# ScalarE's loop back-edge moved from between groups to between the second and third tile of a group

## The chip, the core and the metric

The kernel runs on one core of a Trainium2 chip. The metric is device time in microseconds. Five engines run their own instruction streams and meet at semaphores only: TensorE (PE), VectorE (DVE), ScalarE (ACT), GpSimd (POOL) and SyncE (SP), which issues most DMAs. Before the change the kernel takes 840.57 us, the median of three runs (840.33 to 841.09).

## The reference, cut to what matters

512 samples each look up 32 embedding rows of 32 numbers. Two layers of a compressed interaction network follow, and then a small dense network.

```python
for W in filters:                                  # two layers, 128 maps each
    z = einsum('bhd,bmd->bhmd', x0, prev)          # x0: 512 x 32 x 32
    cur = relu(einsum('bpd,pn->bnd', z.reshape(b, h * m, d), W[0]))
    prev = cur; outs.append(cur)
z = sum(concatenate(outs, axis=1), axis=-1)
h = relu(concatenate([z, dense_ctx], axis=1) @ W_top1 + b_top1)
y = relu(h @ W_top2 + b_top2) @ W_top3
```

Nearly all of the work is the second layer: for every sample, place d, field h of 32 and map n, a sum over 128 maps of the first layer, multiplied by the embedding x0[b, h, d], and then summed over h.

## The kernel before, in words

The samples are cut into 128 tiles of four samples (128 rows of sample and place), and four tiles make a group (`TG` is 4), so there are 32 groups. For each tile, PE computes the second layer's product before the multiplication by the embedding: eight banks of PSUM, k from 0 to 7, each with four fields of 128 maps. One bank takes three matmuls of 512 columns (`layer1`, L921, L922, L929: high and low halves of float32 numbers). PSUM has six such banks in a ring (`RING`). PE writes bank n only when the reader of bank n-6 is done; those are the waits at L910 and L911, on `act_scaled` and `dve_scaled`.

ACT reads five of a tile's eight banks (k = 0, 1, 3, 5, 6): four instructions a bank multiply 128x128 by the embedding and write `prod` (`scale`, L577). DVE reads the other three (k = 2, 4, 7), and adds its products onto ACT's of the bank named in `PARTNER` (L746), so that it waits for ACT as well. POOL folds `prod` (L447), and DVE reduces the rest of it (L758).

Between these, each engine makes ready the next groups. The first layer of the next group is 13 matmuls of PE in each group, three in the second tile and ten in the third (`Z_USED_AT`, L972). ACT has, in a group, five instructions `split_z` (L538; three in the first tile, two in the second), one `rectify_parts` (L561, `c_parts`, at the end of the second tile) and one `rectify_hi` (L555, in the fourth tile). So ACT's extra work stands in the first two tiles of a group and PE's in the third.

All engines run `over_groups` (L103). Groups 0 and 1 are written out. Groups 2 to 28 are a loop of nine iterations with three groups each, and groups 29 to 31 are written out again. The order of work of each engine is the order of the code in `body`; there is no scheduler. At the end of an iteration each engine's own sequencer adds one to the loop's register and branches back (L108), eight times. Nothing makes the engines turn over together, apart from the semaphores of the work. In the stream of ACT the loop is 375 instructions, in that of DVE 317.

Of the kernel before, what the change touches and what calls it, by code (L numbers as in the profile page):

```python
# [39 lines left out]
TG = 4  # L40
# [8 lines left out]
SLOTS = 3  # L49
# [50 lines left out]
        engine.wait_ge(semaphore, value)  # L100


def over_groups(engine, body):  # L103

    body(Group(0, 0), 0)
    body(Group(0, 1), 1)
    loops = (GROUPS - 2) // SLOTS - 1
    with engine.Fori(0, loops) as i:  # L108
        for r in range(2, 2 + SLOTS):
            body(Group(i, r), None)  # L110
    for g in range(2 + SLOTS * loops, GROUPS):
        body(Group(g // SLOTS, g % SLOTS), g)


LAST = Group((GROUPS - 1) // SLOTS, (GROUPS - 1) % SLOTS)
# [2 lines left out]
def tower(nc, ids_and_bounds, copy_of, ones_of_b, picks, table, dense_x, dense_w, w0a, w0b, w1, wt1, wt2, bt2, wt3, y):  # L118
    ctx = ExitStack()
    with ctx:  # L120
# [193 lines left out]
        def _(sp):  # L314
# [76 lines left out]
            def body(g, number):  # L391
                if number is None or number > 1:
                    write_h1(g.plus(-2))
                if number is None or number + SLOTS < GROUPS:
                    send(g.plus(SLOTS), number is None or number + SLOTS + 1 < GROUPS)
                    fetch(g.plus(SLOTS))

            over_groups(sp, body)
            for s in range(SLOTS):
                sp.wait_ge(h1_written[s], 16 * BT * (len(range(s, GROUPS - 2, SLOTS)) + 1))  # L400
# [7 lines left out]
        def _(pool):  # L408
# [64 lines left out]
            def body(g, number):  # L473
                more = number is None or number + 1 < GROUPS
                folds_late = number is None or number < GROUPS - 1
                for u in range(TG):
# [49 lines left out]
                    if (number, u) == (GROUPS - 2, 3):  # L526
                        nc.gpsimd.tensor_copy(dense_x_r[:, :], dense_x_sb[:, :]).then_inc(top_hi_ready, 1)
                        nc.gpsimd.tensor_copy(dense_w_r[:, :], dense_w_sb[:, :]).then_inc(top_hi_ready, 1)

            over_groups(pool, body)  # L530

        @block.scalar
        def _(act):
            def split_z(g, k):

                act.wait_ge(z_ready, g.times(KP, k + 1))
                wait(act, l0_done, g.times(1))
                nc.scalar.activation(z_hi[:, k, :], z[:, k, :], ACT.Copy,  # L538
                                     scale=copy_sb[:, 0:1] if k == LASTK else 1.0).then_inc(z_hi_ready, splits_at_once(g))

            def round_z(tiles, hi_ready, count):

                nc.scalar.activation(by_tile(z_hi[:, LASTK, :])[:, tiles], by_tile(z[:, LASTK, :])[:, tiles], ACT.Copy,
                                     scale=copy_sb[:, 0:1]).then_inc(hi_ready, count)

            def rectify_first(at, out_of, hi_ready):

                nc.scalar.activation(c_hi[:, 0, at], out_of[:, at], ACT.Relu).then_inc(hi_ready, 1)

            def rectify_hi(g):  # L550

                act.wait_ge(l0_done, g.times(1, 1))
                if not isinstance(g.i, int) or g.i > 0:
                    act.wait_ge(h0_done, g.times(1, 1 - SLOTS))
                nc.scalar.activation(c_hi[:, g.r, :], ps_c[:, :], ACT.Relu).then_inc(c_hi_ready, 1)  # L555

            def rectify_parts(g):

                act.wait_ge(reduced, g.times(TG * HALVES, TG * HALVES))
                wait(act, c1_ready, g.times(1))  # L560
                nc.scalar.activation(c1_parts[:, :, :], csum[:, g.r, :, :], ACT.Relu).then_inc(parts_rectified, 1)  # L561

            def rectify_end(u):

                act.wait_ge(reduced, LAST.times(TG * HALVES, (u + 1) * HALVES))
                nc.scalar.activation(c1_end[:, u, :], csum[:, LAST.r, :, u], ACT.Relu).then_inc(end_rectified, 1)

            def scale(g, u, k):

                if k == ACT_BANKS[u][0]:  # L570
                    if u == 0:
                        act.wait_ge(es_ready, g.times(1, 1))
                    wait(act, reduced, g.times(TG * HALVES, (u + 1 - BUFS) * HALVES))
                act.wait_ge(y_ready, g.times(TG * NK, u * NK + k + 1))
                for j in range(HB):
                    h, place = HB * k + j, place_of(u, k) + j
                    last = nc.scalar.activation(prod[:, buffer_of(g, u), place // 2, :, place % 2],  # L577
                                                ps_y[:, bank_of(g, u, k), j * N:(j + 1) * N], ACT.Copy,
                                                scale=es[:, g.r, u, h:h + 1])
                last.then_inc(act_scaled, 1)  # L580

            def round_w1(banks):

                for k in banks:
                    act.wait_ge(w1_in[k * W1_LOADS // NK], 16)
                    nc.scalar.activation(w1_hi[:, k * HB:(k + 1) * HB, :], w1_raw[:, k * HB:(k + 1) * HB, :],
                                         ACT.Copy).then_inc(w1_hi_ready, 1)
# [16 lines left out]
            rectify_first(FIRST_TILE, ps_h1, first_c_hi)  # L604
            round_w1((4, 5))

            def body(g, number):
                more = number is None or number + 1 < GROUPS
                for u in range(TG):
                    for k in range(NK):  # L610
                        if number == 0 and (u, k) == (0, 3):
                            act.wait_ge(z_ready, KP)
                            round_z(slice(1, TG), z_hi_ready, SPLIT)
                            round_w1((6, 7))
                        if number == 0 and (u, k) == (0, 5):
                            act.wait_ge(l0_done, 1)
                            rectify_first(OTHER_TILES, ps_c, c_hi_ready)
                        if number == GROUPS - 1 and (u, k) in A1_HI_AT:
                            rectify_a1(A1_HI_AT.index((u, k)))
                        if k in ACT_BANKS[u]:  # L620
                            scale(g, u, k)
                        for (n, chunk), at in (Z_HI_AT_FIRST if number == 0 else Z_HI_AT).items():
                            if at == (u, k) and (number is None or number + n < GROUPS):
                                split_z(g.plus(n), chunk)
                        if (u, k) == (1, 6) and number != 0:
                            rectify_parts(g.plus(-1))
                        if number == GROUPS - 1 and (u, k) in ((2, 7), (3, 6)):
                            rectify_end(u - 2)
                        if more and (u, k) == (3, 1):
                            rectify_hi(g.plus(1))  # L630
# [6 lines left out]
            def rectify_a1(j):  # L637

                act.wait_ge(mm_top, j + 1)
                nc.scalar.activation(base_late[:, j, :], ps_c[:, late], ACT.Copy).then_inc(base_kept, 1)  # L640
                nc.scalar.activation(a1_hi[j][:, early], ps_c[:, early], ACT.Relu).then_inc(a1_hi_ready, 1)

            over_groups(act, body)


            rectify_end(2)
# [509 lines left out]
```

## Time and profile before

| what | value |
|---|---|
| median of three runs | 840.57 us |
| the profiled execution's own time | 840.71 us |
| its span | 838.9 us |
| PE busy | 829.7 us, 99% of the span |
| ACT busy | 795.8 us, 95% |
| DVE busy | 789.4 us, 94% |
| POOL busy | 733.2 us, 87% |
| granted TensorE clock | full over the whole span |

The profile is one execution. Its span runs from the first to the last instruction, and 1.8 us of the execution's time lie outside. A busy PE means here that matmuls follow each other without a gap that the profile counts. Sequencer instructions (branches, register arithmetic, semaphore waits) are not counted as busy, but the trace has their times. An engine's sequencer runs ahead of the engine and leaves instructions queued for it. A name such as ACTq is ACT's sequencer.

### The profile page before, as it was taken

To read this page: it belongs to the slowest core of one execution; us is meant where nothing else is said; L and a number is where in the kernel's file an instruction comes from. 1 tells how busy PE (TensorE), PEld (TensorE's weight loads), DVE (VectorE), ACT (ScalarE), POOL (GpSimd) and SP (SyncE) were. 2 spreads that over 40 slices of the span, in tenths; PEclk is the share of its full clock that TensorE was granted. 3 is DMA by queue.
4 is the path that set the end of the run, shared out by engine and by line. 5 is a ranking of instruction groups with operands and counts; after the bars stand their busy time and mean duration, and the time that the engine had idled before them with its cause. 6 is when DMAs were issued, how large, how long until landed. Compare 5 with 4: busy or idle time off the path is not lost.

```text
span 838.9 us, 18877 instructions
## 1 busy us (share of the span) xinstructions
PE 829.7 (99%) x3627; PEld 676.8 (81%) x3627; DVE 789.4 (94%) x2061; ACT 795.8 (95%) x2808; POOL 733.2 (87%) x550
## 2 busy tenths in 40 slices
PE   8999999999999999999999999999999999999999
PEld 6688888788788878878887888788788878888887
DVE  7799999999999989999999999999999989999996
ACT  4799999999999999999999999999999999999995
POOL 5898999899899989998998999899899989999860
PEclk9999999999999999999999999999999999999999
DMA  5541222221132221222231222231122221132000
GB/s 152 176 141 37 61 81 84 83 85 43 54 79 84 83 85 38 59 84 80 83 85 39 57 83 82 82 85 55 41 81 83 83 85 45 51 86 76 1 14 1
DMA packets 62144, 60.52 MB, mean 72 GB/s; under 512 B 26203, under 2 KB 37083, under 8 KB 62078
## 3 DMA queue, kind: packets, MB, share of 16 engines
q1 hardware_dynamic: 57982, 57.80, 23.4%
q0 software_dynamic: 4096, 2.11, 1.7%
q14 instruction: 57, 0.47, 0.2%
q8 instruction: 9, 0.15, 0.1%
HBM read 55.51 MB, written 4.31 MB: 71 GB/s over the span
## 4 chain that ended last, share of the span: by engine, by line
PE 87%; ACT 7%; issue 3%; DMA 1%; POOL 1%; ACTq 0%; SPq 0%; DVE 0%
PE ps_y L921 25%; PE ps_y L929 25%; PE ps_y L922 25%; ACT prod L577 6%; PE ps_c L904 3%; PE ps_c L903 3%; PE ps_c L902 3%; POOL gat L458 1%; PE ps_c L900 1%; ACT z_hi L538 1%; DMA w_raw<-w 1%; PE ps_c L891 0%; DMA gat<-table,rows 0%; PE ps_y L1025 0%; DMA ids_and_bounds_sb<-ids_and_bounds 0%
## 5 line engine op out<-in xcount | busy, mean ns | idle before, releaser
L577 ACT ACTIVATE prod<-ps_y,es 128x128 f32<-128x128 f32 x2560 | 752.3, 687 | 22.6 <-PE ps_y L929 21.9
L746 DVE SCALAR_TENSOR_TENSOR prod<-ps_y,es,prod 128x128 f32<-128x128 f32 x1536 | 423.4, 341 | 35.3 <-ACT prod L577 26.9
L921 PE MATMUL ps_y<-w_hi,c_both 128*128 128x512 f32 x1024 | 404.2, 395 | 4.8 <-ACT prod L577 3.7
L929 PE MATMUL ps_y<-w_hi,c_both 128*128 128x512 f32 x1024 | 399.0, 390 | 0.0
L922 PE MATMUL ps_y<-w_lo,c_both 128*128 128x512 f32 x1024 | 398.7, 389 | 0.0
L447 POOL TENSOR_TENSOR prod<-prod 128x768 f32<-128x768 f32 x128 | 248.9, 1945 | 50.5 <-DVE prod L746 39.4
L758 DVE TENSOR_REDUCE csum<-prod 128x64 f32<-128x896 f32 x256 | 276.2, 1080 | 0.1
L921 PEld LDWEIGHTS ps_y<-w_hi,c_both 128*128 128x128 f32 x1024 | 192.4, 188 | 51.4 <-ACT prod L577 8.6
L922 PEld LDWEIGHTS ps_y<-w_lo,c_both 128*128 128x128 f32 x1024 | 192.5, 188 | 42.4 <-issue 1.0
L929 PEld LDWEIGHTS ps_y<-w_hi,c_both 128*128 128x128 f32 x1024 | 192.2, 188 | 41.7
L437 POOL TENSOR_TENSOR z<-first,second 128x512 f32<-128x512 f32 x155 | 200.0, 1301 | 0.0
L425 POOL TENSOR_TENSOR z_lo<-z,z_hi 128x512 fp32r<-128x512 f32 x121 | 156.0, 1300 | 1.2 <-issue 1.2
L416 POOL DMA_INDIRECT gat<-table,rows_now x116 | 110.6, 954 | 31.1 <-issue 25.2
L538 ACT ACTIVATE z_hi<-z 128x512 fp32r<-128x512 f32 x120 | 112.7, 939 | 0.0
L904 PE MATMUL ps_c<-z_lo,w_hi 128*128 128x512 f32 x120 | 48.8, 407 | 0.0
L903 PE MATMUL ps_c<-z_hi,w_lo 128*128 128x512 f32 x120 | 46.6, 388 | 0.0
L902 PE MATMUL ps_c<-z_hi,w_hi 128*128 128x512 f32 x120 | 46.5, 388 | 0.0
L731 DVE TENSOR_REDUCE h<-c_both 128x1024 f32 (+1 forms) x32 | 38.7, 1208 | 0.0
L538 ACT ACTIVATE z_hi<-z,copy_sb 128x512 fp32r<-128x512 f32 x31 | 36.6, 1180 | 0.0
L561 ACT ACTIVATE c_parts<-csum 128x512 f32<-128x512 f32 x31 | 34.6, 1117 | 0.0
L902 PEld LDWEIGHTS ps_c<-z_hi,w_hi 128*128 128x128 f32 x120 | 22.5, 188 | 4.7
L903 PEld LDWEIGHTS ps_c<-z_hi,w_lo 128*128 128x128 f32 x120 | 22.5, 188 | 4.7
(122 smaller groups left out, 299.4 us busy)
## 6 DMA issues: line engine op xcount, KB each, us to landing
second<-et_scratch SPq DMA_DIRECT2D x155, 256.0 KB, 4.4
first<-et_scratch SPq DMA_DIRECT2D x31, 256.0 KB, 3.3
et_scratch<-gat SPq DMA_DIRECT2D x62, 64.0 KB
w_raw<-w SPq DMA_DIRECT2D x4, 512.0 KB, 4.8
h_scratch<-h_sums SPq DMA_DIRECT2D x120, 2.0 KB
gat<-table,rows_now POOLq DMA_INDIRECT x116, 2.4
wt_sb<-wt SPq DMA_DIRECT2D x2, 512.0 KB
rows_now<-rows SPq DMA_DIRECT2D x30, 2.0 KB, 1.8
```

The source lines that it names most:

```text
L416: pool.indirect_dma_start(out=gat[:, g.r, u * D:(u + 1) * D], out_offset=None, in_=table, in_offset=bass.IndirectOffsetOnAxis(ap=rows_now[ ...
L425: nc.gpsimd.tensor_tensor(z_lo[:, k, :], z[:, k, :], z_hi[:, k, :].bitcast(F32), ALU.subtract).then_inc(z_lo_ready, LOWS if unsplit(g) else 1)
L437: nc.gpsimd.tensor_tensor(z[:, k, :], first[:, :], second[:, k, :], ALU.mult).then_inc(z_ready, 1)
L447: nc.gpsimd.tensor_tensor(high, high, low, ALU.add).then_inc(folded, 1)
L538: nc.scalar.activation(z_hi[:, k, :], z[:, k, :], ACT.Copy, scale=copy_sb[:, 0:1] if k == LASTK else 1.0).then_inc(z_hi_ready, splits_at_o ...
L577: last = nc.scalar.activation(prod[:, buffer_of(g, u), place // 2, :, place % 2], ps_y[:, bank_of(g, u, k), j * N:(j + 1) * N], ACT.Copy, ...
L746: last = nc.vector.scalar_tensor_tensor(out=summed, in0=ps_y[:, bank_of(g, u, k), j * N:(j + 1) * N], scalar=es[:, g.r, u, h:h + 1], in1=s ...
L758: nc.vector.tensor_reduce(csum[:, g.r, maps, u], prod[:, buffer_of(g, u), fields_folded(g, u) // 2:SCALED // 2, maps, :].rearrange("p a n ...
L903: nc.tensor.matmul(ps_c[:, :], w0_lo[:, k, :], high, start=False, stop=False)
L921: nc.tensor.matmul(out, hi, w_hi, start=True, stop=False)
L922: nc.tensor.matmul(out, hi, w_lo, start=False, stop=False)
L929: nc.tensor.matmul(out, lo, w_hi, start=False, stop=True).then_inc(y_ready, 1)
```

## The change

`over_groups` gets a further argument, `cut`. With `cut` the body of a group is split by tiles: the first `cut` tiles of group 2 are written out ahead of the loop, each pass of the loop does the remaining tiles of its three groups and the first `cut` tiles of the group behind each, and group 29's remaining tiles stand behind the loop. ACT alone calls it with `cut` 2; the other four engines call it as before, and their instructions stay as they were. ACT's instructions come in the same sequence as before; only the loop's boundary is laid elsewhere among them.

```diff
-def over_groups(engine, body):
+def over_groups(engine, body, cut=0):
     body(Group(0, 0), 0)
     body(Group(0, 1), 1)
+    if cut:
+        body(Group(0, 2), 2, range(cut))
     loops = (GROUPS - 2) // SLOTS - 1
     with engine.Fori(0, loops) as i:
         for r in range(2, 2 + SLOTS):
-            body(Group(i, r), None)
+            if cut:
+                body(Group(i, r), None, range(cut, TG))
+                body(Group(i, r + 1), None, range(cut))
+            else:
+                body(Group(i, r), None)
     for g in range(2 + SLOTS * loops, GROUPS):
-        body(Group(g // SLOTS, g % SLOTS), g)
+        if g == 2 + SLOTS * loops and cut:
+            body(Group(g // SLOTS, g % SLOTS), g, range(cut, TG))
+        else:
+            body(Group(g // SLOTS, g % SLOTS), g)
...
-            def body(g, number):
+            def body(g, number, tiles=range(TG)):
                 more = number is None or number + 1 < GROUPS
-                for u in range(TG):
+                for u in tiles:
...
-            over_groups(act, body)
+            over_groups(act, body, 2)
```

The end of the loop in ACT's stream, before: the last rows are the fourth tile of the iteration's last group, and behind the branch stands group 29, written out.

```order
L555 ACTIVATE c_both<-ps_c 128x512
L574 REGISTER_ALU
L577 ACTIVATE prod<-ps_y,es 128x128 x4
L574 REGISTER_ALU
L577 ACTIVATE prod<-ps_y,es 128x128 x4
L574 REGISTER_ALU
L577 ACTIVATE prod<-ps_y,es 128x128 x4
L108 REGISTER_ALU
L108 COMPARE_AND_BRANCH
```

Here the branch stands behind the last three banks of a fourth tile.

The same place in ACT's stream now: the last rows are the end of a second tile (the lines are nine higher in the new file; L570 is `rectify_parts`).

```order
L547 ACTIVATE z_hi<-z,copy_sb 128x512
L583 REGISTER_ALU
L586 ACTIVATE prod<-ps_y,es 128x128 x4
L568 REGISTER_ALU
L570 ACTIVATE c_parts<-csum 128x512
L110 REGISTER_ALU
L110 COMPARE_AND_BRANCH
L586 ACTIVATE prod<-ps_y,es 128x128 x28
```

The branch has moved from behind three banks of a fourth tile to behind `c_parts` of a second one. The first rows of the loop in ACT's stream, before, with the fused register operations (ISA) that stand between the loop's head and the first `scale` of a group:

```order
L108 UNCONDITIONAL_BRANCH
L108 ISA
L100 ISA
L574 ISA
L577 ACTIVATE prod<-ps_y,es 128x128 x4
L536 ISA
```

Three register operations (L108, L100, L574) stand between the branch's target and the first `scale`.

The first rows of the loop in ACT's stream now, where a third tile begins:

```order
L110 UNCONDITIONAL_BRANCH
L110 ISA
L583 ISA
L586 ACTIVATE prod<-ps_y,es 128x128 x4
L583 REGISTER_ALU
L586 ACTIVATE prod<-ps_y,es 128x128 x4
```

At the head one register operation fewer stands ahead of the first `scale` (the wait for the group's embeddings, L100, belongs to a first tile). The loop stays at 375 instructions, and begins 54 instructions later in ACT's stream.

## Rows read from the trace of the kernel before

**Rows 1.** The page, part 1: busy time of each engine.
```profile
PE 829.7 (99%) x3627; PEld 676.8 (81%) x3627; DVE 789.4 (94%) x2061; ACT 795.8 (95%) x2808; POOL 733.2 (87%) x550
```
**Rows 2.** Waits of PE (engine, tile, line, whom: us in total, times, longest).
```profile
PE ps_y L921 <- ACT prod L577: 3.7, 8, 0.6
PE ps_y L940 <- DVE z_lo L661: 1.5, 1, 1.5
PE ps_y L921 <- POOL w_lo L465: 1.1, 2, 0.8
```
**Rows 3.** Loop branches, line L108 (count: ns min/median/max, first and last start).
```profile
L108 PEldq COMPARE_BRANCH  x9: 76/208/239, 143.9 to 746.7; - x9
L108 ACTq COMPARE_BRANCH  x9: 40/45/45, 145.7 to 748.6; - x9
```
**Rows 4.** Windows of four successive groups of PE; the third follows a turn.
```profile
core 0: us, PE busy (x) PEld busy (x) DVE busy (x) ACT busy (x) POOL busy (x), PEclk, DMA share, GB/s
171.72:196.56 24.84, 24.84 (x111) 20.47 (x109) 24.44 (x67) 24.77 (x90) 23.18 (x18) 1.00 0.25 72
196.56:221.40 24.84, 24.84 (x111) 20.47 (x109) 24.32 (x66) 24.50 (x89) 23.12 (x18) 1.00 0.25 73
221.40:247.06 25.66, 25.21 (x111) 20.32 (x109) 23.53 (x62) 24.23 (x89) 22.30 (x17) 1.00 0.26 70
247.06:271.90 24.84, 24.84 (x111) 20.47 (x109) 24.45 (x66) 24.78 (x90) 23.13 (x18) 1.00 0.25 72
```
**Rows 5.** Chain of waits at the first turn (start us, us, what).
```profile
145.71 0.04 ACTq L108
145.75 0.02 issue
145.77 1.53 ACT prod L577 x5
147.30 1.12 issue
148.42 0.06 ACTq L108
148.48 0.04 issue
148.52 0.04 ACTq L100
148.55 0.04 issue
148.59 0.04 ACTq L574
148.63 0.05 issue
148.68 0.15 ACT prod L577
...
151.43 0.50 PE ps_y L921
```
**Rows 6.** DMA queues from 145.72 to 221.0, one iteration (queue: packets, MB, share).
```profile
q14 instruction: 5, 0.04, 0.2%
```
**Rows 7.** Timeline of ACT about the new place, 210.1 to 217.2 ([idle before]).
```profile
210.17 1.12 ACT L561 ACTIVATE c_parts<-csum 128x512 f32<-128x512 f32 x1
210.69 5.78 ACT L577 ACTIVATE prod<-ps_y,es 128x128 f32<-128x128 f32 x20
216.81 0.64 ACT L577 ACTIVATE prod<-ps_y,es 128x128 f32<-128x128 f32 x2 [0.34 <-PE ps_y L929]
```
**Rows 8.** ACT's sequencer just before and behind that c_parts, L559 and L574.
```profile
L559 ACTq ALU_OP  x1: 35/35/35, 207.7 to 207.7; - x1
L574 ACTq ALU_OP  x1: 35/35/35, 207.8 to 207.8; - x1
```
**Rows 9.** Timeline of ACT to 211.6: the first bank of that third tile.
```profile
210.69 1.64 ACT L577 ACTIVATE prod<-ps_y,es 128x128 f32<-128x128 f32 x4
```
**Rows 10.** Timeline of PE: that bank's last matmul, and its bank's next use.
```profile
208.59 0.39 PE L929 MATMUL ps_y<-w_hi,c_both 128*128 128x512 f32 x1
...
214.31 0.40 PE L921 MATMUL ps_y<-w_hi,c_both 128*128 128x512 f32 x1
```

## The prediction

> **What bounds the kernel now.** I read the page's busy times first: PE is busy for 829.7 of 838.9 us [rows 1], so what PE waits for is all that a change of order can win. The waits of PE come next. Outside the start there is one kind: eight times, 3.7 us in total, a matmul of L921 waits for ACT's `scale` [rows 2]. Eight is also the number of times that the loop branches back; nine branches are recorded, and the last falls through [rows 3]. To price these eight places I compare groups of PE. Three of the four groups shown take 24.84 us with PE busy in all of it, and the one that follows a turn takes 25.66 [rows 4] (the 109 matmuls of a group appear as 111, with the neighbours that reach in). PE's branches recur every (746.7 - 143.9) / 8 = 75.35 us [rows 3], and three groups without a wait are 74.52 us. So a turn costs 0.83 us, more than the wait that is listed, because the matmuls on both sides of it are stretched too. Everything else in the loop already runs at PE's pace.
>
> The chain of waits shows where the 0.83 us comes from [rows 5]. ACT's sequencer takes the branch at 145.71. Five instructions are then still queued for the engine, and the last of them ends at 147.30. The sequencer's next instruction comes at 148.42, 2.7 us behind the branch, and the first `scale` of the new iteration at 148.68. The chain calls the gap "issue", so no semaphore ended it. In each iteration five packets of instructions are loaded [rows 6]. The plain reading is that the branch goes to code which must be fetched again. ACT thus stands still, while PE goes on into its ring until, at 151.43, it needs a bank that ACT has not read.
>
> **The change, part by part.** No work is added or removed. ACT branches eight times as before, and executes the same ACTIVATEs in the same order; two tiles more are written out ahead of the loop and two fewer behind it, which on ACT's side only drops or adds register operations that its sequencer does ahead of time. SP, POOL, DVE and PE keep their streams, so no DMA is issued behind other work than before.
>
> *What goes.* The stall at the group's boundary: 8 x 0.83 = 6.6 us of PE.
>
> *What comes.* The same branch, behind `c_parts` of a second tile. Two things decide its price: how long the queue behind the branch keeps ACT busy, and how much PE can wait for.
>
> The queue first. In a group without a turn near it, the sequencer prepares `c_parts` at 207.7 and is past it at 207.8 [rows 8], while `c_parts` itself runs from 210.17 and the next `scale` starts at 210.69 [rows 7]. The branch will stand where the instruction of 207.8 stands, a register addition later, so about 207.9. The engine then has work for 210.69 - 207.9 = 2.8 us. At the old place it had 1.3 us: five instructions at 0.25 us of spacing (the 20 of [rows 7] take 5.0 us but for the last one's tail) from 145.77. The reason for the difference is that in a second tile ACT is behind PE, having just done its `split_z` instructions, and `y_ready` does not hold its sequencer back; in a fourth tile it has caught up, and its sequencer stands at a wait for PE shortly before the branch.
>
> From branch to first `scale` took 148.68 - 145.71 = 2.97 us [rows 5]. At the new head one register operation is missing, 0.07 us by the spacing from 148.52 to 148.59 in the same rows, which leaves 2.90. ACT would then stand for 2.90 - 2.8 = 0.1 us. The bounds: nothing, if the fetch is shorter, and 2.90 - 1.3 = 1.6 us, if the queue were as short as at the old place. The loop's code lies 54 instructions further on, so the pieces that are fetched are cut differently, and the rows cannot say whether that makes the wait shorter or longer. I take 0.1 us, since the rows of this very place give the 2.8.
>
> PE next. The first bank of the third tile is finished by PE at 208.59 + 0.39 = 208.98 [rows 10]. ACT reads it with four instructions from 210.69 to 212.33 [rows 9]. PE writes that bank again six banks later, at 214.31 [rows 10], because it does ten first-layer matmuls within this tile. So ACT can be late by 214.31 - 212.33 = 1.98 us before PE feels it. The delay also dies within the tile: the 20 instructions of it end, and ACT waits 0.34 us for PE [rows 7]. A stall of 0.1 us costs PE nothing, and one of 1.6 us would nothing or nearly so. If all cover were gone, 2.9 us of stall would cost 2.9 - 1.98 = 0.9 us a turn, a little more than now.
>
> What is late next? With the stall gone, the groups behind a turn run as the others do, in which PE is busy all the time and DVE for 24.32 to 24.45 of 24.84 us [rows 4]. DVE is close, but it does not bind: those groups follow each other in pairs now, without a wait.
>
> The Trainium skill, page "Runtime: NRT & Kernel Launch", section "Instruction fetch mechanics", says that a taken branch whose target is not among the loaded pages forces a fetch before execution goes on. The 2.7 us without a releaser agree with it. Read strictly, the rule speaks against this change: the fetch stays wherever the branch stands, and by it alone the time would stay at 840.6. The rule is about the sequencer, and whether the engine and PE notice is what the rows above decide; the case in which they do is the second rival.
>
> *Sum.* 840.71 (the profiled execution) - 6.6 + 0 = 834.1 us. The median of the runs is 0.14 below that execution, which gives 833.9; I forecast 834.0.
>
> **Rivals.**
> 1. *Part of it stays.* ACT's late start reaches DVE, which adds its products to ACT's and has only 0.4 to 0.5 us a group to recover. For it: DVE's share in [rows 4]. Against it: 0.1 us is small beside that. With some 0.3 us of PE lost a turn, 840.7 - 8 x 0.53 = 836.5.
> 2. *No change.* The eight waits belong to the group boundary and not to ACT's branch: PE, DVE and POOL turn over there too, and would hold PE in the same manner. For it: they do branch there, PE at 143.9 [rows 3]. Against it: the chain goes from PE back to ACT's branch and to no other [rows 5]. Time 840.6.
> 3. *Slower.* The sequencer is held just ahead of the branch. `rectify_parts` waits for two semaphores of DVE, and stands directly ahead of the branch now. If DVE were late with them, the engine would run dry first and the fetch would follow in full. It decides from the point at which the queue behind the branch lasts less than 2.90 - 1.98 - 0.83 = 0.1 us; a sequencer that comes 0.5 us after the queue is empty gives a stall of 3.4 us and a loss of 3.4 - 1.98 = 1.4 us a turn, so 840.7 + 8 x (1.4 - 0.83) = 845. Against it: at 207.7 to 207.8 the sequencer passes this wait without a stop [rows 8].
>
> **How the numbers follow.** The forecast has 0.84, the first rival 0.08, the second 0.05, the third 0.03. The forecast's own range is 833.2 to 835.2 (a turn's price of 0.8 to 0.9 us, the spread of the runs, and up to 0.1 us of stall left a turn). With the first rival the range becomes 833.2 to 836.8. Less than 0.2%, which is 1.7 us, cannot be told from no change here; both the forecast and the first rival are beyond that, so faster has 0.91, the same 0.06 and slower 0.03.
>
> **What would show it.** In the trace after the change the waits of PE for `scale` are gone or far below 3.7 us; all groups of PE in the loop take 24.84 us, and PE's branches recur every 74.5 us. ACT's branch comes about 2.8 us ahead of the first `scale` behind it that the old queue would have allowed, and ACT's gap there is under 0.4 us. The packets of instructions are still loaded. The forecast is wrong if PE waits for ACT in third tiles, if the groups that follow PE's own branch still take 25.6 us, or if ACT's sequencer stands ahead of `c_parts`.

## The result, and the profile after

The changed kernel takes 835.58 us, the median of six runs (833.88 to 838.49), beside 841.09 for the kernel before (840.33 to 842.84). The ratio is 0.9931 [0.9909, 0.9952]: faster by 0.7%. The forecast was 834.0 with a range from 833.2 to 836.8; the median lies in that range, but above the forecast's own 833.2 to 835.2. The profiled execution took 833.88 us, of which 832.1 are its span. Some executions here, of the kernel before too (847 to 849 us), have a lower granted clock (0.993 to 0.998 on the mean) and take longer, so where it matters a median over the executions at full clock is given as well.

The page of the kernel after, parts 1, 3 and 4 (busy times, the instruction queue, the chain that ended last by engine):

```profile
PE 826.4 (99%) x3627; PEld 677.9 (81%) x3627; DVE 788.0 (95%) x2061; ACT 795.7 (96%) x2808; POOL 733.1 (88%) x550
...
q14 instruction: 57, 0.47, 0.2%
...
PE 97%; DMA 1%; POOL 1%; issue 0%; SPq 0%; DVE 0%; ACT 0%
```

Beside [rows 1] nothing was saved in work: ACT and POOL are busy as long as before. The chain is PE's for 97% of it, where ACT's branch stood in it before [rows 5]. The waits of PE of the kernel after, in the columns of [rows 2]:

```profile
PE ps_y L949 <- DVE z_lo L670: 1.5, 1, 1.5
PE ps_y L930 <- POOL w_lo L474: 1.3, 2, 1.0
PE ps_y L955 <- ACT z_hi L605: 0.9, 1, 0.9
```

The eight waits for `scale` (L586 in the new file) are gone; what is left belongs to the start, and from 40 to 800 us PE waits for nothing. The branches of the kernel after, from 140 us on (ACT's first eight):

```profile
L110 PEldq COMPARE_BRANCH  x9: 76/208/239, 143.7 to 739.9; - x9
L110 ACTq COMPARE_BRANCH  x8: 45/45/45, 157.3 to 679.0; - x8
```

PE's branches now recur every (739.9 - 143.7) / 8 = 74.53 us, against 75.35 in [rows 3]. ACT still branches eight times inside the loop, and the packets on the instruction queue are still 57. Four successive groups of PE after the change, which hold two of ACT's turns (157.3 and 231.8), in the columns of [rows 4]:

```profile
145.99:170.83 24.84, 24.84 (x110) 20.47 (x109) 23.34 (x62) 24.21 (x88) 22.44 (x18) 1.00 0.25 72
170.83:195.67 24.84, 24.84 (x110) 20.47 (x109) 24.45 (x66) 24.78 (x90) 23.06 (x18) 1.00 0.24 72
195.67:220.51 24.84, 24.84 (x110) 20.47 (x109) 24.32 (x66) 24.52 (x89) 23.13 (x18) 1.00 0.25 73
220.51:245.35 24.84, 24.84 (x110) 20.47 (x109) 23.18 (x61) 24.05 (x88) 22.36 (x17) 1.00 0.26 72
```

All four take 24.84 us. DVE and ACT do less in the first and the last of them, where the turn is, and PE doesn't notice. From the first group that PE runs at its pace (46.63) to the last (791.85) it is 745.22 us, where the kernel before took 751.90 (46.75 to 798.65). That is 6.68 of the 6.83 us between the two profiled executions; PE's earlier start is another 0.12.

One thing is not as forecast. ACT's timeline about its second turn (start, duration, in brackets the idle time ahead):

```profile
232.51 1.18 ACT L547 ACTIVATE z_hi<-z,copy_sb 128x512 fp32r<-128x512 f32 x1
233.13 1.61 ACT L586 ACTIVATE prod<-ps_y,es 128x128 f32<-128x128 f32 x4
234.13 1.12 ACT L570 ACTIVATE c_parts<-csum 128x512 f32<-128x512 f32 x1
236.03 1.15 ACT L586 ACTIVATE prod<-ps_y,es 128x128 f32<-128x128 f32 x4 [0.79 <-DVE csum L767]
```

The branch is at 231.84, so `c_parts` starts 2.29 us behind it, and the next `scale` 4.19 us behind it. I measure the gap from the start of `c_parts` to the start of the next `scale`. It is 236.03 - 234.13 = 1.90 us here and 210.69 - 210.17 = 0.52 without a turn [rows 7]. Over the eight turns the `scale` comes 3.19 to 4.19 us behind the branch, not 2.90, and the gap is 0.91 to 1.91, so ACT is late by 0.4 to 1.4 us, not by 0.1, and the forecast's sign of a gap under 0.4 us, taken as this delay, is met at one turn of the eight. The words "<-DVE csum" name an operation that ended at 235.82, shortly before; it is not what ACT waited for, since it ends 3.96 to 3.98 us behind the branch at all eight turns, and at five of them the `scale` starts before that. It is the sequencer that came late, as its own records there show:

```profile
L583 ACTq ALU_OP  x2: 35/35/35, 231.1 to 236.1; - x2
L583 ACTq FUSED_REGOPS  x1: 37/37/37, 236.0 to 236.0; - x1
```

Between its branch at 231.84 and 235.86 the sequencer has no record at all, on L583, the line that stands at the loop's new head, or on another.

Where does this delay end? DVE adds to ACT's products and waits for them. DVE's timeline of the kernel after, around and behind the turn at 529.93 (gap 1.89), first the tile at the turn, then `z_lo`, then the same place of the next group:

```profile
535.30 1.13 DVE L755 SCALAR_TENSOR_TENSOR prod<-ps_y,es,prod 128x128 f32<-128x128 f32 x4 [1.41 <-ACT prod L586]
...
549.32 0.68 DVE L734 TENSOR_TENSOR z_lo<-z,z_hi 128x512 fp32r<-128x512 f32 x1
...
559.69 1.13 DVE L755 SCALAR_TENSOR_TENSOR prod<-ps_y,es,prod 128x128 f32<-128x128 f32 x4 [0.45 <-ACT prod L586]
```

DVE stands for 1.41 us where it normally stands for 0.45. The 0.96 us that it is late stay with it, since it has no further idle time until `z_lo` at 549.32. `z_lo` ends at 550.00, and PE's next first-layer matmuls, which use it, begin with L911 at 550.25:

```profile
550.25 0.38 PE L911 MATMUL ps_c<-z_hi,w_hi 128*128 128x512 f32 x1
```

So a gap of 1.9 us is just about what this turn can bear.

### The profile page after: what moved, and what is told of

It reads as the page before. It is cut to its first block, busy times and chain, and to the rows that moved or that the text cites. A ratio compares the mean times of both kernels' runs of the same rounds, so it can differ in the third digit from the quotient of the medians.

```text
span 832.1 us, 18877 instructions
## 1 busy us (share of the span) xinstructions
PE 826.4 (99%) x3627; PEld 677.9 (81%) x3627; DVE 788.0 (95%) x2061; ACT 795.7 (96%) x2808; POOL 733.1 (88%) x550
## 4 chain that ended last, share of the span: by engine, by line
PE 97%; DMA 1%; POOL 1%; issue 0%; SPq 0%; DVE 0%; ACT 0%
PE ps_y L930 28%; PE ps_y L938 28%; PE ps_y L931 28%; PE ps_c L913 3%; PE ps_c L912 3%; PE ps_c L911 3%; POOL gat L467 1%; PE ps_c L909 1%; DMA w_raw<-w 1%; PE ps_c L900 0%; DMA gat<-table,rows 0%; PE ps_y L1034 0%; DMA ids_and_bounds_sb<-ids_and_bounds 0%; POOL w_lo L474 0%; PE ps_y L1036 0%
## 5 line engine op out<-in xcount | busy, mean ns | idle before, releaser
L586 ACT ACTIVATE prod<-ps_y,es 128x128 f32<-128x128 f32 x2560 | 752.5, 639 | 15.9 <-PE ps_y L938 12.3
L911 PE MATMUL ps_c<-z_hi,w_hi 128*128 128x512 f32 x120 | 46.6, 388 | 0.0
L570 ACT ACTIVATE c_parts<-csum 128x512 f32<-128x512 f32 x31 | 34.4, 1111 | 0.0
L911 PEld LDWEIGHTS ps_c<-z_hi,w_hi 128*128 128x128 f32 x120 | 22.5, 188 | 4.9
```

What stands on the lines that cost most here:

```text
L911: nc.tensor.matmul(ps_c[:, :], w0_hi[:, k, :], high, start=(k == 0), stop=False)
```

## The experiments

The theory: the 0.83 us of a turn is ACT's code being loaded again behind the branch. The price is what ACT's gap has above a patience of the place, by PE's ring of banks or by DVE. Rivals: the turn-over of the other engines costs it, or the shift of the code by 54 instructions does, or any place but the group's end does as well.

**The change once more (e8_change_again).** No edit; it was run again to see how far its executions differ.

> The change itself, beside the three others on the same chip: 834 to 836 us by the median. If the loop is at PE's pace in every execution, its spread is that of the kernels without reload. Whether its profile shows waits of PE for scale tells if some executions lose time at the turn.

835.81 us (834.18 to 843.84, 12 runs) beside 840.71, ratio 0.9955 [0.9925, 0.9985]. The profiled execution took 836.12, and 2.2 of the 2.24 us to the first one are in the loop: 747.45 in place of 745.22. Its eight gaps are 1.28, 1.33, 1.66, 2.10, 3.02, 2.57, 1.77 and 2.15 us. The group in which a turn lies and the one behind it together lost 0, 0, 0, 0.19, 1.13, 0.68, 0 and 0.25 us. That is the gap less 1.89 to 1.91, where this is above nothing. The two groups of the turn at 531.25, in windows as in [rows 4]:

```profile
519.93:544.85 24.92, 24.92 (x111) 20.39 (x110) 22.59 (x59) 23.46 (x85) 21.96 (x17) 1.00 0.24 72
544.85:570.29 25.44, 25.44 (x110) 20.20 (x109) 25.00 (x68) 25.44 (x93) 23.34 (x19) 1.00 0.24 70
```

ACT's timeline at that turn:

```profile
533.54 1.11 ACT L570 ACTIVATE c_parts<-csum 128x512 f32<-128x512 f32 x1
536.11 1.16 ACT L586 ACTIVATE prod<-ps_y,es 128x128 f32<-128x128 f32 x4 [1.46 <-PE ps_y L938]
```

The gap is 536.11 - 533.54 = 2.57 us. DVE's timeline there, and at the next `z_lo`:

```profile
537.31 1.13 DVE L755 SCALAR_TENSOR_TENSOR prod<-ps_y,es,prod 128x128 f32<-128x128 f32 x4 [2.09 <-ACT prod L586]
...
551.33 0.68 DVE L734 TENSOR_TENSOR z_lo<-z,z_hi 128x512 fp32r<-128x512 f32 x1
```

DVE stood for 2.09 us, worked 14 us without a pause, and finished `z_lo` at 552.01. PE's L911, due at 552.00 by the usual spacing of 0.23, came at 552.16. Another part of the loss lies at banks that DVE reads, where PE's matmuls from 546 to 549 are stretched. In the turn with a gap of 2.10 it all lies at the first matmuls behind `z_lo`. Most of the loss is thus in the group *behind* the turn and no wait of the page names it: the second row has a PE that is busy for all of 25.44 us, with the matmuls further apart.

**The reload taken away, at the old place and the new (e4_no_reload_old_place, e5_no_reload_new_place).** ACT's code comes in packets of 8 KB, and in the middle of a pass the next one starts 124 to 134 of ACT's records after the last, so I count 128 instructions to a packet. By that count a loop of 375 touches four of them in either kernel; five are loaded in every pass [rows 6], so with one read ahead all come anew. Instructions that only count a spare semaphore, ahead of the loop, move it to where it should touch three. For e4 the loop is cut behind a whole group, so that ACT turns over at a group's end as before, but one group (24.8 us) later than the other engines do.

```diff
+            for _ in range(67):          # e5; in e4 23
+                act.sem_inc(spare, 1)
             act.wait_ge(picks_in, 16)
...
-            over_groups(act, body, 2)
+            over_groups(act, body, 4)    # e4 alone
```

> ACT's loop turns over between groups, as before, but begins one group later and 23 semaphore increments later, so that its 375 instructions should lie in three pieces of 128 in place of four (an estimate: by the Trainium skill, page Runtime: NRT & Kernel Launch, section Instruction fetch mechanics, 256 instructions are 16 KiB; the packets of the profile have 8.2 KB, so 128 instructions). Theory (the turn costs time because code is loaded again): no or far fewer instruction packets in an iteration, ACT's first scale follows the branch without a gap, PE does not wait, 833.9 us, and runs differ by less than 0.5 us. Rival (the group boundary itself, where all engines turn over, costs the 0.83 us): PE's groups behind a turn still take 25.6 us and the time is 840.5 us.

> The change as it is, with 67 increments of an unused semaphore ahead of ACT's first work, so that the loop should lie in three pieces of code and stay loaded, as it did at the old place with 23 increments and one group more ahead of the loop. Theory: no instruction packets in the loop's iterations for ACT, the first scale follows c_parts without a gap; PE lost nothing at this place before either, so the time does not fall: 834 to 835 us, the same as the change alone, since runs differ by their start and not by the loop. Rival (runs of the change differ because the load varies, and some lose time by it): 833.9 us with a spread under 0.5 us, and some 1.5 us below the change alone run beside it.

e4: 834.72 us (833.66 to 837.07), ratio 0.9928 [0.9914, 0.9941]; the spread is wider than its theory has it. e5: 836.01 (833.74 to 848.36), ratio 0.9949 [0.992, 0.9979]. In both profiles all groups take 24.84 us (745.20 us for the loop). The DMA queues of e4 from 171 to 245, nearly a pass of its loop (packets, MB, share):

```profile
q1 hardware_dynamic: 5400, 5.14, 23.7%
q0 software_dynamic: 384, 0.20, 1.9%
```

ACT's timeline of e4 about its turn at 170.9:

```profile
168.72 0.65 ACT L565 ACTIVATE c_both<-ps_c 128x512 fp32r<-128x512 f32 x1
169.20 4.31 ACT L587 ACTIVATE prod<-ps_y,es 128x128 f32<-128x128 f32 x16
```

The instruction queue of [rows 6] is absent, and ACT goes through its turn without a gap; its first `scale` comes 0.30 us behind the branch. The other engines turn over where they did, and PE loses nothing: the 6.7 us came with the reload. ACT does not turn over together with them here, so e4 alone leaves open whether both have to meet; the kernel before and e1 (below) answer that. In their sixteen turns, where all engines turn over at one boundary and the gap between `scale` starts is 1.59 to 2.10 us, the group loses that gap less 1.14, to within 0.05 us. A turn without a gap would lose nothing by that. Over the executions at full clock the medians of e5's series are 840.53 before, 835.62 for the change (9 executions) and 834.35 for e5 (5). By these the reload still costs the change 1.3 us, as e5's rival has it (though its spread is 1.4 us), and the new place saves the rest; over all executions, 835.81 and 836.01, the two cannot be told apart.

**The old place with the code shifted by 54 (e1_old_place_shifted).** The kernel before, with 54 such instructions ahead of ACT's work, so that its loop lies in the packets as that of the change does.

```diff
+            for _ in range(54):
+                act.sem_inc(spare, 1)
             act.wait_ge(picks_in, 16)
```

> ACT's loop stays at the old place (between groups), but 54 increments of an unused semaphore stand ahead of it, so that its code lies where it lies after the change. Theory (the branch waits for code; data transfers at the new place hold that load up): at the old place there are hardly any transfers, so the instruction packet starts 0.3 to 0.5 us behind the branch and the first scale comes about 2.0 to 2.3 us behind it, against 2.97 before, because no other instruction packet is under way just then; ACT's gap is about 0.9 us, PE loses 0.0 to 0.3 us a turn, and the time is 834 to 837 us. Rival (the 54 instructions made the load longer after the change): the first scale comes 3.2 to 4.2 us behind the branch here too, PE loses about 1 us or more a turn, and the time is 840 to 845 us.

839.02 us (838.01 to 841.35), ratio 0.9982 [0.9972, 0.9991]: neither theory's number. ACT's first `scale` comes 2.64 to 2.89 us behind the branch (2.93 to 3.16 before). ACT's timeline at the second turn (branch at 221.0):

```profile
219.56 3.03 ACT L578 ACTIVATE prod<-ps_y,es 128x128 f32<-128x128 f32 x11
223.90 1.15 ACT L578 ACTIVATE prod<-ps_y,es 128x128 f32<-128x128 f32 x4 [1.31 <-PE ps_y L932]
```

The window of e1 from 221.67 to 247.00, most of the group behind that turn:

```profile
221.67:247.00 25.33, 25.02 (x110) 20.20 (x109) 23.37 (x61) 24.02 (x88) 22.04 (x17) 1.00 0.25 71
```

By PE's own starts the groups behind a turn take 25.24 to 25.52, so 0.40 to 0.68 are lost. In the kernel before, two packets start ahead of the first `scale`, 0.3 to 0.6 and 0.9 to 1.4 us behind the branch, and I take the first for one that is read ahead; with the shift there is only one, at 0.9. The mean gap between `scale` starts at the turns fell from 1.98 to 1.72 us. 8 x 0.26 is 2.1 us, and the time fell by 2.0 (841.04 before, in that series). The shift thus makes some three tenths of a turn's 0.83 us, and it did not make the change's loads longer.

**Other places (e3_cut_one, e2_cut_three).** The loop cut behind the first or the third tile, `over_groups(act, body, 1)` or `3`.

> ACT's loop turns over between the first and the second tile. Theory: the transfers of a group have not begun there, or only just, so the packet starts within 0.6 us and the first scale comes 2.0 to 2.5 us behind the branch; ACT is 1.2 us behind PE there, the queue lasts some 2 us, and ACT's gap is 0 to 0.5 us; PE has 0.6 to 1.3 us to spare in a second tile: 833.9 to 834.5 us. Rival (as after the change, 3.2 to 4.2 us from branch to scale): gap 1.2 to 2.2 us in a tile in which ACT cannot catch up, PE loses 0.5 to 1.5 us a turn, 838 to 846 us.

> ACT's loop turns over between the third and the fourth tile. By then the transfers of the group are over. Theory: the instruction packet starts 0.3 to 0.6 us behind the branch, the first scale comes 2.0 to 2.4 us behind it; ACT has caught up with PE there, so the queue lasts only about 1.3 us and ACT's gap is 0.7 to 1.1 us; PE's ring has about 2 us to spare in a fourth tile, so PE loses nothing: 833.9 us with hardly any spread. Rival (what counts is how far ACT is behind PE, the load takes 3.2 to 4.2 us anywhere but at the old place): gap 1.9 to 2.9 us, PE loses 0 to 0.9 us a turn, 834 to 841 us.

e3: 834.58 us (833.82 to 835.02), ratio 0.9921 [0.9907, 0.9935]; first `scale` 2.60 to 2.83 us behind the branch, gap 0.8 to 1.1, all groups 24.84: the time is nearly the theory's, though the load takes longer than it has. e2: 852.32 (850.31 to 855.73), ratio 1.0134 [1.0110, 1.0158]: slower than before, and a plain miss. First `scale` 2.57 to 4.79 us behind the branch, with a queue of 0.94 us. ACT of e2 behind its first branch, at 164.97:

```profile
165.66 0.52 ACT L586 ACTIVATE prod<-ps_y,es 128x128 f32<-128x128 f32 x1
169.10 2.18 ACT L586 ACTIVATE prod<-ps_y,es 128x128 f32<-128x128 f32 x8 [2.93 <-PE ps_y L938]
```

The gap is 3.44 us, and the two groups there lost 1.85. In seven turns the loss is the gap less 1.6; the eighth is disturbed by a stop of DVE (last section).

What makes the load long can be read from the instruction queue's share in a short window with one code packet in it: share x 16 engines x window is the time that the packet took. The DMA queues (packets, MB, share) of e3 from 152.3 to 155.0:

```profile
q1 hardware_dynamic: 85, 0.04, 5.1%
q14 instruction: 1, 0.01, 1.3%
```

Of the change, its first profile, from 529.9 to 534.0:

```profile
q1 hardware_dynamic: 618, 1.13, 83.7%
q14 instruction: 1, 0.01, 2.0%
```

Of the change, its second profile (e8), from 455.6 to 460.8:

```profile
q1 hardware_dynamic: 743, 1.28, 81.1%
q14 instruction: 1, 0.01, 2.8%
```

Of e2, from 544.7 to 550.5:

```profile
q0 software_dynamic: 46, 0.03, 4.3%
q14 instruction: 1, 0.01, 3.1%
q1 hardware_dynamic: 107, 0.00, 1.0%
```

The packet takes 0.6 us in e3, 1.3 and 2.3 in the change, where 1.1 to 1.3 MB of `second` are loaded beside it, and 2.9 in e2, where next to nothing is moved. There a row of tiny writes to `h_scratch` goes ahead of it: four writes of 2 KB in 512 packets of 16 bytes, of which the window holds the end (the 107 packets that make 0.00 MB). In seven of the eight turns the last of them starts 0.7 to 0.9 us ahead of the branch; the one turn without them has a packet of 0.3 us. The gathers of queue 0 are not the cause, since packets of 1.9 and 2.3 us (branches at 164.97 and 393.57) have none beside them. The packet also starts later in the change: 1.5 to 2.5 us behind the branch, against 0.9 to 1.1 in e3. In the change these writes come 3.9 us or more behind the branch, after the packet, so that beside it there are the loads alone.

**The reload taken away from e2 (e7_cut_three_no_reload).** Cut 3 and 46 counting instructions ahead of the loop.

> The turn between the third and the fourth tile, which took 852 us, with 46 increments of an unused semaphore ahead of ACT's first work, so that the loop should lie in three pieces and stay loaded. Theory (all of the loss there is the reload: ACT's gap of 1.6 to 3.8 us at a point where it has no queue and much to do next): no instruction packets in the iterations, no gap, 834 to 835 us. Rival (turning over there costs something beside the reload, as by the work in front of the fourth tile): 840 us or more.

834.48 us (834.36 to 836.57), ratio 0.9925 [0.9899, 0.9951], against 1.0134 with the reload. All groups take 24.84, as the theory has it. Cutting behind a third tile does no harm by itself; all that e2 lost came with the reload.

**The tiny writes moved away from e2's turn (e9_cut_three_writes_moved).** Cut 3, and SP issues the writes of `h_scratch` (`write_h1`) behind its writes of `et_scratch` (`send`) in place of ahead of them, so that they fall at another time.

```diff
+                more = number is None or number + SLOTS < GROUPS
+                if more:
+                    send(g.plus(SLOTS), number is None or number + SLOTS + 1 < GROUPS)
                 if number is None or number > 1:
                     write_h1(g.plus(-2))
-                if number is None or number + SLOTS < GROUPS:
-                    send(g.plus(SLOTS), number is None or number + SLOTS + 1 < GROUPS)
+                if more:
                     fetch(g.plus(SLOTS))
...
-            over_groups(act, body, 2)
+            over_groups(act, body, 3)
```

> The turn between the third and the fourth tile with its reload, as in the run that took 852 us, but SyncE issues the four small writes of sums (2 KB each, in pieces of a few bytes) ahead of the six loads of 256 KB in place of behind them, so that they no longer stand a microsecond ahead of ACT's branch. Theory (these writes held the load of code up: packets of 1.0 to 2.8 us in seven turns, and of 0.3 us in the one turn without them): the packets of instructions take 0.3 to 0.6 us and start 0.9 us behind the branch, the first scale comes 2.4 to 2.8 us behind it, ACT's gap is 1.5 to 1.9 us, PE loses 0 to 0.4 us a turn, and the time is 834 to 838 us. Rival (the writes have nothing to do with it; the load is slow there for another reason, or ACT's place alone costs the time): packets of 1 to 2.8 us as before, and 850 us.

The load behaves as the theory says: 2.59 to 2.66 us from branch to `scale` in all eight turns, where e2 had up to 4.79. The window 171.1 to 174.8 holds one packet and nothing else, of 0.008 x 16 x 3.7 = 0.5 us:

```profile
q14 instruction: 1, 0.01, 0.8%
```

But the time is 897.03 us (894.18 to 899.89), ratio 1.0669 [1.0586, 1.0753], and neither expectation has it. PE's waits name another cause:

```profile
PE ps_c L913 <- DVE z_lo L736: 41.0, 8, 5.7
```

Eight stops of 4.6 to 5.7 us, at DVE's `z_lo`. So the part on the load holds, and the edit brought another trouble, which the last section shows; why DVE's `z_lo` met it in every pass here was not looked into.

**A later restart at the new place (e6_late_restart).** Cut 2, and 22 counting instructions at the head of ACT's loop, which the sequencer goes through behind the load. This doses the delay.

```diff
     with engine.Fori(0, loops) as i:
+        if opening:
+            opening()                    # ACT: 22 x act.sem_inc(spare, 1)
```

> The change, with 22 increments of an unused semaphore at the head of ACT's loop: its sequencer comes about 1.5 us later to the first scale behind each turn, where its queue is empty. ACT's gap becomes 2.2 to 3.2 us in place of 0.7 to 1.7. Theory (PE has 1.98 us to spare for that bank, and every microsecond beyond is lost): PE waits for ACT at third tiles, 0.2 to 1.2 us a turn, and the time is 836 to 844 us, most likely 840. Rival (ACT's start at this place hardly matters to PE): 834 us.

846.58 us (843.39 to 857.80), ratio 1.0071 [1.0036, 1.0105]: slower than before, beyond the upper end of what was expected. The gaps are 2.62 to 4.27 us. The turn at 232.69 has the largest; its two groups, in windows:

```profile
221.36:247.94 26.58, 25.38 (x111) 20.31 (x109) 22.59 (x59) 23.42 (x86) 21.93 (x17) 1.00 0.25 67
247.94:273.39 25.45, 25.39 (x110) 20.18 (x109) 25.08 (x68) 25.44 (x93) 23.40 (x19) 1.00 0.25 70
```

They lost 1.74 + 0.61 = 2.35 us, and 4.27 - 1.92 is the same. The rule found in e8, with 1.92 in place of its 1.89 to 1.91, gives 0.76, 2.35, 1.52, 2.08, 0.88, 1.15 and 0.70 us for the seven turns of this profile that nothing else disturbs, and they measured 0.76, 2.35, 1.51, 2.06, 0.86, 1.15 and 0.68. With the eighth it gives 11.3 us. The profiled execution is the longest of its series (857.80), as it holds two further stops at `z_lo`; the executions at full clock have a median of 844.9, and 833.9 + 11.3 is 845.2. A delay at the new place is free up to a gap of 1.92 us and then costs its full length.

## Why the prediction was right, point by point

*What bounds the kernel.* Right. PE's waits were all there was to win, and the experiments without a reload end at PE's pace, 24.84 us a group.

*What goes: 8 x 0.83 = 6.6 us.* Right in size and cause. The loop became 6.68 us shorter in the profiled execution, and e4 shows that it is the reload and not the place of the turn by itself. The second rival, that the other engines turn over there too and hold PE, is refuted by e4, where they still do and PE loses nothing; that ACT's gap alone prices the turn where it turns over together with them is shown by the sixteen turns of the kernel before and e1.

*The price of the new place: a stall of 0.1 us.* This term of the sum was mis-sized, though inside the bound of 1.6 us that the prediction gave, in the first profile. It measured 0.4 to 1.4 us there and up to 2.5 in the second profile. Two rows were combined that don't belong together. The queue of 2.8 us was nearly right (branch to `c_parts` 2.29, plus 0.52, is 2.81). The 2.97 us from branch to `scale` was carried over from the old place, and the time of a load depends on what the DMA queues do just then: 2.6 to 2.8 us in the quiet place of e3, 3.2 to 5.3 at the new place, where `second` is loaded. The prediction asked about where the code is cut (0.3 us a turn, e1), and not about what else is being moved. The rows for it were there, in the DMA view of the new place.

*PE's slack of 1.98 us hides it.* Right for PE's ring, and too generous for the turn. The slack and the 0.52 without a turn make a gap of 2.50, and the group of the turn itself loses 0.08 us at a gap of 2.57 and 0.55 at 3.02 (e8), 1.74 at 4.27 (e6). But DVE's `z_lo`, 14 us later, bears only 1.92, which is 1.40 of delay. The prediction's "The delay also dies within the tile" is where it goes wrong: it dies for ACT, but DVE has taken it over by then. "1.6 us would nothing or nearly so" is true by the rule (0.2 us); the 0.9 for a stall of 2.9 us should have been 1.5. That the first profile lost nothing is in part luck: its longest delay, 1.39 us, falls just inside the 1.40.

*The first rival, that part of it stays through DVE.* It was given 0.08 and a time of 836.5, and it is what the second profiled execution does (836.12, 2.25 us lost in four turns, most of it in this way). That DVE "has only 0.4 to 0.5 us a group to recover" was the right row; the prediction let it go since it took the stall as 0.1 us. The median of 835.58 lies between the forecast and this rival: in the first profile no load was too slow, in the second four were. What also spreads the runs is PE's start, 46.5 to 47.8 us in these profiles, which the change does not touch.

*The third rival, slower.* Its mechanism (the sequencer held ahead of the branch) was not seen, as the branch stands 2.29 us ahead of `c_parts`. A slower kernel was near in another way: one tile further on (e2) it was slower than before.

Of the Trainium skill, the page "Runtime: NRT & Kernel Launch", section "Instruction fetch mechanics", says that a taken branch to code that isn't loaded has to fetch it first. e4, e5 and e7 agree: with all of the loop's code held, there is no packet and no gap. The strict reading in the prediction, that by this alone the time would stay, fails: the fetch stayed and the time fell.

What stays open is why the load starts later and takes longer in the new place than in e3. That it goes with the loads of `second` was seen at all turns, but no run moved those loads.

Over all executions no kernel here is shown to be faster than the change; over those at full clock e5 and e7 (834.35 and 834.46) are 1.2 to 1.3 us below it in the same series. In the profiles of e3, e4, e5 and e7 no group takes more than 24.84 us.

## What to carry to other kernels

A loop's branch on a busy engine costs the reload of its code, less what the engine has queued and what the next engines can bear; look at all three where you put it, and at what the DMA queues do just then. Better is a loop whose code stays loaded: look whether the instruction queue has packets in the middle of the loop, and if it has, try where the loop lies before you move work. A delay can cost time a group later, where no wait names it, so compare the starts of groups and not only waits.

## What the runs showed of the hardware

*A code load can be slow where next to nothing is moved.* A packet of 8 KB took 0.3 to 0.6 us at the turns of the kernel before, e1 and e3, 0.3 to 2.3 in the change, beside loads at some 250 to 280 GB/s, and up to 2.9 us (e2) 1.6 us or more behind the last of a row of four tiny writes. With these moved away (e9) it took 0.3 to 0.5 us. One such write alone does no harm: in the kernel before a packet that runs beside 65 to 81 of its 16-byte packets takes 0.5 to 0.6 us. Why writes that have gone by hold up a load is not shown.

*A DVE operation can stand behind a stream of POOL's.* In e2 one group took 31.27 us. DVE's timeline there:

```profile
686.18 6.33 DVE L734 TENSOR_TENSOR z_lo<-z,z_hi 128x512 fp32r<-128x512 f32 x1
```

POOL's timeline in the same stretch:

```profile
686.46 1.82 POOL L456 TENSOR_TENSOR prod<-prod 128x768 f32<-128x768 f32 x1
688.25 1.26 POOL L446 TENSOR_TENSOR z<-first,second 128x512 f32<-128x512 f32 x1
689.47 2.48 POOL L434 TENSOR_TENSOR z_lo<-z,z_hi 128x512 fp32r<-128x512 f32 x2
698.37 1.86 POOL L456 TENSOR_TENSOR prod<-prod 128x768 f32<-128x768 f32 x1 [6.41 <-DVE prod L755]
```

`z_lo` takes 0.69 us at most in the kernel before, and 6.33 here: it ends 0.6 us after POOL's last operation in a row that has next to no gap, and that began before it (a `z` of POOL from 685.20). There are eleven such places, one in e2, two in e6 and eight in e9, with 6.3 to 7.1 us each, and in all of them `z_lo` ends 0.5 to 0.6 us behind the last of five or six operations of POOL; those of e9 make its 41 us of waits. The Trainium skill, page "SBUF — State Buffer", section "Who interferes with whom", has it that a DVE instruction with two SBUF inputs contends with a GpSimd instruction that reads SBUF, and that their shared pair of ports is an exclusive lock. The rows agree that DVE is held up, and show that it can last for a whole row of POOL's instructions.

*The granted clock fell behind a stop of PE.* The same place, in windows of 5 us (columns as in [rows 4]; the granted clock is the last but two):

```profile
686.00:691.00 5.00, 1.89 (x9) 1.23 (x7) 5.00 (x3) 5.00 (x19) 5.00 (x5) 1.00 0.07 21
691.00:696.00 5.00, 3.44 (x9) 2.72 (x10) 4.92 (x9) 0.41 (x1) 0.95 (x1) 0.66 0.81 257
696.00:701.00 5.00, 5.00 (x24) 4.08 (x22) 4.58 (x12) 4.39 (x15) 2.63 (x2) 1.00 0.21 59
```

PE stood for 3.1 of the first 5 us and 1.6 of the next, in which the granted clock was 0.66 on the mean, so part of that time at the lower level (1.2 GHz); it was at 2.4 GHz again in the window after. In the changed kernel no such stop is seen, and the page has the full clock throughout.
